# Self-attention of a fused block on one core: output projection behind the query projection, transposes ahead of the sums, and another order at both ends

## The chip, the cores and the metric

One core of one Trainium2 chip runs the whole block as one program. The metric is device time in microseconds (us), median of three executions. The engines are named as in the profile: PE (TensorE matmuls; PEld are its weight loads), DVE (VectorE), ACT (ScalarE), POOL (GpSimd) and SP (SyncE, which issues the transfers).

## The reference

The input x is 32 sequences of 32 tokens with 512 channels (1024 rows). Three layers follow each other, each added to x:

```python
x = x + xattn(layernorm(x), ctx, ctx)        # 16 heads of 32, 257 keys per sequence
x = x + attn(layernorm(x))                   # self-attention in each sequence of 32
x = x + ffn(layernorm(x))                    # nine experts, one chosen per token

# attn
q, k, v = x @ Wqkv.T + bqkv
q = rms_norm(q); k = rms_norm(k)             # per head: q / sqrt(mean(q*q) + 1e-6)
out = softmax(q k^T / sqrt(32)) v
return out @ Wproj.T + bproj

# ffn
x_mixed = mk[0]*x[s-1] + mk[1]*x[s] + mk[2]*x[s+1]
scores  = tanh(x_mixed @ Wo1 + bo1) @ Wo2 + bo2
path p  = (x_mixed @ W1[p] + b1[p]) @ W2[p] + b2[p]
return layernorm(x + the path with the highest score) * gamma + beta
```

All of it is float32. Each float32 product with 512 channels is made of three fp32r matmuls on operands that are split into a high and a low part (high times high, low times high, high times low).

## The kernel before, in words

**Tiles.** The 1024 rows are eight tiles of 128 rows (`NT` = 8); `NH` = 4 tiles are a half. `x_nat` keeps x in rows, `O_T` keeps the transposed output of cross-attention and later the mixed input of the experts. A projection of one tile (`project`, line 1094, by `three`, line 92) is 4 channel blocks of 3 matmuls of 128x512. "Splitting" means that ACT copies the high part (fp32r) and DVE or POOL subtracts it from the source, which gives the low part.

**Self-attention as a pipeline over turns.** After cross-attention `self_attention_and_experts` runs turns it = 0 to 7 and then some turns written out by hand (turn 8 is `NT`, turn 9 `NT + 1`, turn 10 `NT + 2`). In one turn every engine works on several tiles at once. PE (`body`, line 1206) does in this order: `wo_proj(it + 2)`, the output projection of cross-attention two tiles ahead (`LEAD` = 2, so only in turns 0 to 5); `out_proj(it)`, self-attention's output projection of tile it-3; `qk_transposes(it)`, of q and k of tile it-2, four transposes each; `qkv(it, 0)`, the query projection of tile it-1; `scores(it)` of tile it-2; `qkv(it, 1)` and `qkv(it, 2)`, keys and values; `weighted_sum(it)`; `z2_transposes(it)`, of the normalised x of tile it; `z3_transposes(it)`, of the input of the experts, tile it-3. Turn 2 projects the queries ahead of the q and k transposes.

**What else is in a turn.** Each engine runs its own instruction stream in program order, and they meet only at semaphores. DVE adds projections to x (`take_x1`, `take_x2`), takes the statistics of a layer norm (`x1_stats`, `x2_stats`), moves q, k and v out of PSUM with their bias, sums the squares of q and of k per head (`mean_squares`), multiplies q and k by their inverse norm (`head_norm(tile, 0)` for q, `head_norm(tile, 1)` for k; line 1613), does the softmax (`shift_scores`, `probabilities`) and the low parts `o2_split` and z2's. ACT makes the high parts, the normalised x (`z2_make`, `z3_make`), squares, exponentials, and `mix_parts`, the 12 scaled copies for the mixing of neighbours. POOL (line 1032) takes all inverse roots with a power instruction. Its order in a turn is: `head_norm(1, it-2)`, the roots for the keys (line 1012); `norm1(it)`; `o_rest(it+3)`; `norm3(it-3)`, which waits for `x2_stats(it)` and so for `out_proj(it)`; `with_bproj(it-1)`; `mix(it-4)`, two additions; `head_norm(0, it-1)`, the roots for the queries.

**Who waits for whom, around the change.** The second four transposes of `qk_transposes(it)` wait for `norm_made[1]`, the keys of tile it-2 multiplied on DVE, which waits for POOL's roots, which wait for `mean_squares(it-1, 1)`. On DVE that sum stands behind `head_norm(it-1, 0)` in turn it-1, which waits for POOL's roots for the queries. `out_proj(it)` waits for `o2_split(it-1)` on DVE. The first four transposes wait for z2's low part of tile it-1, since they write into the bank that z2's transposes used.

**Handover.** The weight of self-attention's output projection comes into `raw` while cross-attention's is in use. `weight_split(4)` on ACT and a subtraction of 128x2048 on DVE (line 1699) in turn 1 split it; `out_proj(3)` in turn 3 is its first use.

**Experts.** `gate(hf)` (line 1237) multiplies one half of the mixed input with the gate's weight. It needs `xm_hi`, `xm_lo` (the split mixed input of the half) and `g_hi`, `g_lo` (the split gate weight); POOL makes both low parts in turn 8 (lines 1066 and 1069). Then come `hidden(k)`, `spread(k)` (one matmul that spreads the chosen expert over the partitions, into the one bank `pw0`, evacuated by ACT in `spread_evac`), and `outputs`. The rest of self-attention (turns 9 and 10) is woven in.

**The end.** For the last four tiles DVE adds PE's result (`y_take`), takes statistics, centres and multiplies by gamma (two tiles; POOL does it for the other two, lines 1088 and 1090), takes all four inverse roots by a chain of twelve small instructions (`y_deviations`, `rsqrt`, line 50) and ends with four `y_end`; SP stores each tile.

## Time and profile before

| what | value |
|---|---|
| median of three executions | 794.98 us (794.23 to 797.06) |
| the profiled execution's own time | 793.65 us |
| its span | 791.7 us |
| PE busy | 751.6 us, 95% of the span |
| DVE, ACT, POOL busy | 390.5, 335.9, 187.7 us |
| cross-attention ends, self-attention begins | about 485 us |
| first matmul of the gate | 639.58 us |
| last matmul ends | 780.8 us |

How to read it: the span is the stretch from the first to the last instruction on the chip; the execution's own time is some 2 us more. PE is busy nearly all the time, so what matters are the few places in which it stands still, and what each of them waited for. PE's clock has two levels, 1.2 and 2.4 GHz; a granted clock of 1.00 in a row is the higher one, 0.50 the lower.

### The profile page before, as it was taken

What the parts mean: (1) busy time and instruction counts of PE and PEld (TensorE: products, weight loads), DVE (VectorE), ACT (ScalarE), POOL (GpSimd) and SP (SyncE); (2) the same over time, 40 slices, a digit from 0 to 9 for tenths busy, and PEclk for the clock granted to TensorE, in tenths of its full rate; (3) what the DMA queues carried; (4) which work ended last, traced back from release to release, by engine and by line L of the source; (5) the groups of instructions that cost most, each with busy time, mean ns of one, the idle gap of its engine ahead of it and who ended that gap; (6) DMA issues with size and microseconds to landing.
All of it is one profiled execution on the core that took longest, in us unless ns stands there. A gap on an engine that the chain in (4) does not pass through costs nothing. (4 is left out here: it accounts for less than half of the span.)

```text
span 791.7 us, 20456 instructions
## 1 busy us (share of the span) xinstructions
PE 751.6 (95%) x8258; PEld 587.8 (74%) x8258; DVE 390.5 (49%) x942; ACT 335.9 (42%) x690; POOL 187.7 (24%) x245
## 2 busy tenths in 40 slices
PE   5999999999999999999999999799999989999994
PEld 4777778778877877787788777677877766677673
DVE  5544434343443344243424546756667675633546
ACT  4435444443444344444435455224554545521210
POOL 0001000010010010010100202555777770692002
PEclk9999999999999999999999999999999999999998
DMA  9211110011011101101120114120000022100011
GB/s 331 71 48 55 54 55 23 33 53 53 0 53 53 53 0 53 53 1 52 53 49 4 53 53 108 66 84 3 0 0 4 2 69 80 41 1 0 1 54 53
DMA packets 9471, 37.05 MB, mean 47 GB/s; under 512 B 2633, under 2 KB 2889, under 8 KB 6482
## 3 DMA queue, kind: packets, MB, share of 16 engines
q1 hardware_dynamic: 9426, 36.42, 13.6%
q8 instruction: 31, 0.51, 0.3%
q14 instruction: 14, 0.11, 0.0%
HBM read 34.32 MB, written 2.10 MB: 46 GB/s over the span
## 5 line engine op out<-in xcount | busy, mean ns | idle before, releaser
L94 PE MATMUL pj<-W_hi 128*128 128x512 f32 x512 | 209.1, 408 | 9.7 <-DVE W_lo L594 9.7
L96 PE MATMUL pj<-W_lo,W_hi 128*128 128x512 f32 x512 | 201.2, 393 | 0.0
L95 PE MATMUL pj<-W_hi,W_lo 128*128 128x512 f32 x512 | 200.4, 391 | 0.0
L94 PEld LDWEIGHTS pj<-W_hi 128*128 128x128 f32 x512 | 96.8, 189 | 40.7 <-issue 22.4
L96 PEld LDWEIGHTS pj<-W_lo,W_hi 128*128 128x128 f32 x512 | 96.7, 189 | 21.4
L95 PEld LDWEIGHTS pj<-W_hi,W_lo 128*128 128x128 f32 x512 | 97.0, 189 | 17.9
L235 POOL COPY q_b<-Q_T 128x128 f32 (+1 forms) x32 | 9.3, 291 | 415.8 <-PE tp L358 348.9
L492 ACT ACTIVATE K<-pj,bk 128x512 f32<-128x512 f32 x64 | 44.1, 690 | 136.1 <-PE pj L96 136.1
L654 DVE CUSTOM_DVE_ANT_0 m_flat<-sc,mask 128x257 f32<-128x257 f32 x64 | 25.3, 425 | 115.4 <-PE tp L358 94.1
L507 ACT ACTIVATE p_flat<-m_flat,nmax 128x257 f32<-128x257 f32 x128 | 63.8, 501 | 24.5 <-DVE nmax L654 24.5
L499 ACT ACTIVATE V<-pj 128x512 f32<-128x512 f32 x64 | 38.2, 598 | 73.7 <-PE pj L96 71.8
L594 DVE TENSOR_TENSOR W_lo<-raw,W_hi 128x2048 fp32r<-128x2048 f32 (+1 forms) x19 | 41.4, 2180 | 31.4 <-ACT W_hi L451 31.4
L675 DVE COPY P_T<-tp 128x512 f32<-128x512 f32 x32 | 22.1, 692 | 66.6 <-PE tp L370 66.6
L1012 POOL TENSOR_TENSOR rms<-ms_eps,power 128x16 f32<-128x16 f32 x16 | 48.3, 3020 | 3.6 <-POOL ms_eps L1008 3.6
L663 DVE TENSOR_SCALAR p_flat<-p_flat,rinv 128x257 f32<-128x257 f32 x128 | 42.0, 392 | 1.1
L94 PE MATMUL pw<-W_hi,z_hi 128*128 128x512 f32 x92 | 38.0, 413 | 4.3 <-DVE x_nat L1565 4.3
L95 PE MATMUL pw<-W_hi,z_lo 128*128 128x512 f32 x92 | 36.4, 396 | 0.0
L96 PE MATMUL pw<-W_lo,z_hi 128*128 128x512 f32 x92 | 36.3, 395 | 0.0
L451 ACT ACTIVATE W_hi<-raw 128x2048 fp32r<-128x2048 f32 (+1 forms) x19 | 34.5, 1815 | 3.0 <-DMA raw<-wk_dram 3.0
L370 PE MATMUL tp<-ident,p_flat 128*128 128x128 f32 x256 | 33.1, 272 | 0.7 <-DVE P_T L675 0.7
L370 PEld LDWEIGHTS tp<-ident,p_flat 128*128 128x128 f32 x256 | 29.8, 140 | 4.8 <-issue 0.8
L94 PE MATMUL pt<-xm_hi,W_hi 128*128 128x512 f32 x72 | 29.1, 405 | 0.3 <-DVE bqkv L1737 0.3
(287 smaller groups left out, 1329.3 us busy)
## 6 DMA issues: line engine op xcount, KB each, us to landing
raw<-ctx_dram SPq DMA_DIRECT2D x15, 1024.0 KB, 4.8
raw<-w_dram SPq DMA_DIRECT2D x6, 768.0 KB, 4.9
raw<-w_dram SPq DMA_DIRECT2D x4, 1024.0 KB, 4.8
x_nat<-x_dram SPq DMA_DIRECT2D x2, 1024.0 KB, 11.7
out_dram<-raw SPq DMA_DIRECT2D x8, 256.0 KB, 2.1
raw<-wk_dram SPq DMA_DIRECT2D x2, 512.0 KB, 5.4
p_flat<-ctx_dram SPq DMA_DIRECT2D x2, 512.0 KB, 6.8
m_flat<-wv_dram SPq DMA_DIRECT2D x1, 1024.0 KB, 9.9
```

Of the source, the lines that this page charges most:

```text
L94: eng.matmul(out, a_hi, b_hi, start=first, stop=False)
L95: eng.matmul(out, a_lo, b_hi, start=False, stop=False)
L96: return eng.matmul(out, a_hi, b_lo, start=False, stop=last)
L370: mm = eng.transpose(tp[:, k, g * P:(g + 1) * P], probs[:, j, g, k * P:(k + 1) * P], ident[:, :])
L451: return eng.activation(dst, src, ACT.Copy)
L492: eng.activation(K[:, g, :, 0:SM], pj[g % 2][:, :].rearrange("p (j n) -> p j n", j=2), ACT.Identity, bias=bk[:, g:g + 1]).then_inc(k_out, 1)
L499: eng.activation(V[:, t, :], pj[t % 2][:, :], ACT.Copy).then_inc(v_out, 1)
L507: eng.activation(probs[:, j, g, :], masked[:, j, g, :], ACT.Exp, bias=nmax[:, j, g:g + 1], scale=-1.0, accum_out=psum_[:, j, g:g + 1]).the ...
L594: return eng.tensor_tensor(dst, src, hi.bitcast(F32), ALU.subtract)
L654: eng.tensor_tensor_reduce(masked[:, j, g, :], sc[g][:, 0:SK], mask[:, :], -1.0, BIG, ALU.add, ALU.min, nmax[:, j, g:g + 1]).then_inc(mask ...
L663: eng.tensor_scalar(probs[:, j, g, :], probs[:, j, g, :], rinv[:, j, g:g + 1], None, ALU.mult).then_inc(probs_made, 1)
L1012: eng.tensor_tensor(rms[:, heads], ms_eps[:, heads], power[:, heads], ALU.pow).then_inc(rms_made[i], 1)
```

## The change

Semaphores that only mark what an engine has seen are shared between the two stages (no wait hangs on them), and the unused count `x0_made` is dropped. Beyond that:

- **Turns.** PE does z2's transposes ahead of the weighted sum. In turns 6, 7 and 8, which have no `wo_proj`, `out_proj` stands behind `qk_transposes` and `qkv(it, 0)`. ACT and DVE split z2 ahead of o2. On DVE, `q_evac` stands ahead of `take_x2` in turns 6, 7 and 8.
- **Handover.** DVE's low part of Wproj moves from turn 1 to the end of turn 2, `head_norm(0, 0)` from turn 1 into turn 2 behind `take_x1` and `x1_stats`; ACT splits Wproj behind z2; PE waits for the low part at the end of turn 2.
- **Ahead of the experts.** The mixed input's first half is split tile by tile, on ACT at the end of turns 4 to 7 and on DVE at the end of turns 5 to 8; the gate's weight is split on ACT in turn 6 and on DVE in turn 7. POOL does neither. DVE's turns are written out instead of looped.
- **First experts.** `spread(0)` goes ahead of `weighted_sum(9)`, `out_proj(10)` behind `hidden(2)` and `spread(2)`; ACT and DVE take the evacuations for them ahead of weight splits.
- **End.** POOL takes each of the last four inverse roots by power; tiles 4 and 6 are normalised on ACT, multiplied by gamma on POOL, and added on POOL (4) and on DVE (6); tiles 5 and 7 stay on DVE. The stores follow in the order 4, 5, 7, 6.

The rest of the diff, in the order of the file (SP, POOL, PE, ACT, DVE):

```diff
...
-            for i, t in enumerate((0, 1, 2, 3, 6, 7, 4, 5)):
-                eng.wait_ge(fin, i + 1)
+            for t in range(NH):
+                eng.wait_ge(fin, t + 1)
+                eng.dma_start(out[t], y(t)).then_inc(stored, 16)
+            eng.wait_ge(fin0, 1)
+            eng.dma_start(out[NH], y(NH)).then_inc(stored, 16)
+            for i, t in enumerate((5, 7, 6)):
+                eng.wait_ge(fin, NH + i + 1)
                 eng.dma_start(out[t], y(t)).then_inc(stored, 16)
             eng.wait_ge(stored, 16 * NT)
...
@@ -1062,11 +1069,7 @@
             head_norm(1, NT - 2)
             norm3(NT - 3)
             mix(NT - 4)
-            eng.wait_ge(xmhi, 1)
-            eng.tensor_tensor(xm_lo[:, :, :], O_T[:, :, 0:HT], xm_hi[:, :, :].bitcast(F32), ALU.subtract).then_inc(xmlo, 1)
             head_norm(0, NT - 1)
-            eng.wait_ge(g_split, 1)
-            eng.tensor_tensor(g_lo[:, :, :], g_raw, g_hi[:, :, :].bitcast(F32), ALU.subtract).then_inc(g_split, 1)
             head_norm(1, NT - 1)
             with_bproj(NT - 1)
             norm3(NT - 2)
...
-            for t in range(2):
-                y_t = y(NH + t)
+            def y_root(t):
+                one = slice(t, t + 1)
                 eng.wait_ge(stats_made, NH + t + 1)
-                eng.tensor_scalar(y_t, y_t, mv4[:, t, 0:1], None, ALU.subtract).then_inc(centred, 1)
-                eng.wait_ge(centred, 2 * t + 1)
-                eng.tensor_tensor(y_t, y_t, gamma, ALU.mult).then_inc(centred, 1)
+                eng.tensor_scalar(tmp4[:, one], mv4[:, t, 1:2], LN_EPS, 1.0, ALU.add, ALU.mult).then_inc(root_step, 1)
+                eng.wait_ge(root_step, 2 * t + 1)
+                eng.tensor_tensor(rstd4[:, one], tmp4[:, one], power[:, one], ALU.pow).then_inc(root_step, 1)
+                eng.wait_ge(root_step, 2 * t + 2)
+                if t in (0, 2):
+                    eng.tensor_scalar(shift4[:, one], mv4[:, t, 0:1], rstd4[:, one], -1.0,
+                                      ALU.mult, ALU.mult).then_inc(shift4_made, 1)
+
+            def y_scale(t):
+                eng.wait_ge(normed, t // 2 + 1)
+                eng.tensor_tensor(y(NH + t), y(NH + t), gamma, ALU.mult).then_inc(centred, 1)
+
+            eng.wait_ge(fin, NH)
+            y_root(0)
+            y_scale(0)
+            y_root(1)
+            eng.wait_ge(centred, 1)
+            eng.tensor_tensor(y(NH), y(NH), x_nat[:, NH, :], ALU.add).then_inc(fin0, 1)
+            y_root(2)
+            y_root(3)
+            y_scale(2)
...
-                if isinstance(it, int) and it == 2 and i == 2:
-                    eng.wait_ge(wp_lo, 1)
...
-                if has(it, 3):
-                    out_proj(it)
+                    if has(it, 3):
+                        out_proj(it)
...
+                if not has(it, -LEAD):
+                    out_proj(it)
                 if has(it, 2):
                     scores(it)
                 if has(it, 1):
                     qkv(it, 1)
                     qkv(it, 2)
+                if not isinstance(it, int) or it >= 2:
+                    z2_transposes(it)
                 if has(it, 2):
                     weighted_sum(it)
-                if not isinstance(it, int) or it >= 2:
-                    z2_transposes(it)
+                if isinstance(it, int) and it == 2:
+                    eng.wait_ge(wp_lo, 1)
                 if has(it, 3):
                     z3_transposes(it)
...
@@ -1312,9 +1335,9 @@
 
             steps(eng, body)
 
-            out_proj(NT)
             qk_transposes(NT)
             qkv(NT, 0)
+            out_proj(NT)
             scores(NT)
             qkv(NT, 1)
             qkv(NT, 2)
...
@@ -1329,12 +1352,12 @@
             hidden(0)
             choice_transposes(0)
             hidden(1)
+            spread(0)
             weighted_sum(NT + 1)
-            spread(0)
             spread(1)
-            out_proj(NT + 2)
             hidden(2)
             spread(2)
+            out_proj(NT + 2)
             z3_transposes(NT + 1)
             expert(RING)
...
-                if has(it, 2):
-                    o2_split(it)
-                if isinstance(it, int) and it == 1:
-                    weight_split(4)
                 eng.wait_ge(z2T_done, it + 1)
                 need(eng, qkv_done, 3 * it)
                 eng.activation(z2_hi[:, :, :].rearrange("p c t -> p (c t)"), pt[0][:, :], ACT.Copy).then_inc(z2hi_made, 1)
+                if isinstance(it, int) and it == 1:
+                    weight_split(4)
+                if has(it, 2):
+                    o2_split(it)
                 if has(it, 3):
                     mix_parts(it)
...
-            def xm_split(hf):
-                eng.wait_ge(mix_made, NH * (hf + 1) + 1)
-                if hf:
-                    eng.wait_ge(h_done, E)
-                eng.activation(xm_hi[:, :, :], O_T[:, :, hf * HT:(hf + 1) * HT], ACT.Copy).then_inc(xmhi, 1)
+            def xm_split_tile(u):
+                cols = slice(u * P, (u + 1) * P)
+                eng.wait_ge(mix_made, u + 2)
+                eng.activation(xm_hi[:, :, cols], O_T[:, :, cols], ACT.Copy).then_inc(xmhi, 1)
+
+            def xm_split_rest():
+                eng.wait_ge(mix_made, NT + 1)
+                eng.wait_ge(h_done, E)
+                eng.activation(xm_hi[:, :, :], O_T[:, :, HT:T], ACT.Copy).then_inc(xmhi, 1)
+
+            def g_hi_split():
+                eng.wait_ge(ex_in, 6 * 16)
+                eng.activation(g_hi[:, :, :], g_raw, ACT.Copy).then_inc(g_split, 1)
...
+                if it >= NH:
+                    xm_split_tile(it - NH)
+                if it == NT - 2:
+                    g_hi_split()
...
-            xm_split(0)
             square(NT, 0)
             exps(NT)
-            eng.wait_ge(ex_in, 6 * 16)
-            eng.activation(g_hi[:, :, :], g_raw, ACT.Copy).then_inc(g_split, 1)
...
-            w_split(2)
+            spread_evac(0)
             o2_split(NT + 1)
-            z3_make(NT + 1)
-            spread_evac(0)
             hidden_split(0)
             spread_evac(1)
+            z3_make(NT + 1)
             hidden_split(1)
+            w_split(2)
+            spread_evac(2)
+            hidden_split(2)
...
-            spread_evac(2)
             mix_parts(NT + 1)
-            hidden_split(2)
             w_split(3)
...
                 hidden_split(k)
+            for t in (0, 2):
+                eng.wait_ge(shift4_made, t // 2 + 1)
+                eng.activation(y(NH + t), y(NH + t), ACT.Identity, bias=shift4[:, t:t + 1],
+                               scale=rstd4[:, t:t + 1]).then_inc(normed, 1)
...
+                if isinstance(it, int) and it == 2:
+                    head_norm(it - 2, 0)
                 if has(it, 2):
                     head_norm(it - 2, 1)
+                if not has(it, -LEAD):
+                    q_evac(it)
                 if has(it, 3):
                     take_x2(it)
                     x2_stats(it, ch)
-                if has(it, 1):
+                if has(it, 1) and has(it, -LEAD):
                     q_evac(it)
                 if has(it, 2):
                     shift_scores(it, ch)
@@ -1676,17 +1716,16 @@
...
-                    head_norm(it - 1, 0)
                 elif has(it, 1):
                     k_evac(it)
                     head_norm(it - 1, 0)
                     mean_squares(it, 1)
                     v_evac(it)
-                if has(it, 2):
-                    o2_split(it)
                 eng.wait_ge(z2hi_made, it + 1)
                 eng.tensor_tensor(z2_lo[:, :, :].rearrange("p c t -> p (c t)"), pt[0][:, :],
                                   z2_hi[:, :, :].rearrange("p c t -> p (c t)").bitcast(F32), ALU.subtract).then_inc(z2lo_made, 1)
+                if has(it, 2):
+                    o2_split(it)
...
-                if isinstance(it, int) and it == 1:
+                if isinstance(it, int) and it == 2:
                     eng.wait_ge(whi, 5)
                     eng.tensor_tensor(w_lo[4], raw[:, 0, :].rearrange("p (c n) -> p c n", c=CT), w_hi[4].bitcast(F32),
                                       ALU.subtract).then_inc(wp_lo, 1)
...
+            def xm_lo_tile(u):
+                cols = slice(u * P, (u + 1) * P)
+                eng.wait_ge(xmhi, u + 1)
+                eng.tensor_tensor(xm_lo[:, :, cols], O_T[:, :, cols], xm_hi[:, :, cols].bitcast(F32),
+                                  ALU.subtract).then_inc(xmlo, 1)
...
+            def hidden_made(k):
                 eng.wait_ge(pc_out, k + 1)
                 eng.wait_ge(h_done, k + 1)
                 need(eng, hlo, k - 1)
                 eng.scalar_tensor_tensor(out=h[k % 2], in0=ph(k)[:, :], scalar=b1[:, k % E:k % E + 1],
                                          in1=chosen[k % 2], op0=ALU.add, op1=ALU.mult).then_inc(h_made, 1)
+
+            def hidden_rest(k):
                 eng.wait_ge(hhi, k + 1)
                 eng.tensor_tensor(h_lo[k % RING], h[k % 2], h_hi[k % RING].bitcast(F32), ALU.subtract).then_inc(hlo, 1)
+
+            def hidden_rows(k):
+                hidden_made(k)
+                hidden_rest(k)
...
-            steps(eng, body)
+            for it in range(NT):
+                body(it)
+                if it > NH:
+                    xm_lo_tile(it - NH - 1)
+                if it == NT - 1:
+                    eng.wait_ge(g_split, 1)
+                    eng.tensor_tensor(g_lo[:, :, :], g_raw, g_hi[:, :, :].bitcast(F32), ALU.subtract).then_inc(g_split, 1)
             ch = Chain(eng, step, count["at"])
             head_norm(NT - 2, 1)
+            q_evac(NT)
             take_x2(NT)
             x2_stats(NT, ch)
-            q_evac(NT)
...
             v_evac(NT)
+            xm_lo_tile(NH - 1)
             o2_split(NT)
+            head_norm(NT - 1, 1)
             w_split(0)
-            head_norm(NT - 1, 1)
...
+            hidden_made(0)
             o2_split(NT + 1)
-            hidden_rows(0)
+            hidden_rest(0)
+            hidden_rows(1)
             w_split(2)
-            hidden_rows(1)
+            hidden_rows(2)
             take_x2(NT + 2)
             x2_stats(NT + 2, ch)
             eng.wait_ge(b2_split, 1)
             eng.tensor_tensor(b2_lo, b2, b2_hi.bitcast(F32), ALU.subtract).then_inc(b2_split, 1)
-            hidden_rows(2)
             w_split(3)
...
             for t in range(NH):
                 y_take(1, t)
                 y_stats(1, t)
-                if t == 2:
-                    y_centre(1, t)
-            y_centre(1, NH - 1)
-            y_deviations()
-            for t in (2, 3, 0, 1):
-                if t < 2:
-                    eng.wait_ge(centred, 2 * t + 2)
+                if t == 1:
+                    y_centre(1, 1)
+            y_centre(1, 3)
+            for t in (1, 3):
+                eng.wait_ge(root_step, 2 * t + 2)
                 y_end(1, t)
+            eng.wait_ge(centred, 2)
+            eng.tensor_tensor(y(NH + 2), y(NH + 2), x_nat[:, NH + 2, :], ALU.add).then_inc(fin, 1)
...
```

## Rows read from the trace of the kernel before

**Rows 1.** PE's waits, 484 to 670 us: total, times, longest.
```profile
PE pw L94 <- DVE x_nat L1565: 4.3, 1, 4.3
PE pw L94 <- DVE o_lo L1641: 4.3, 3, 1.4
PE pa L1190 <- DVE e_T L1637: 1.9, 1, 1.9
PE pw L1276 <- ACT sq L1486: 1.7, 1, 1.7
PE pw L94 <- POOL g_lo L1069: 1.4, 1, 1.4
```
**Rows 2.** Stretches: length, PE busy (instructions), granted clock, DMA share, GB/s.
```profile
513.40:517.70 4.30, 4.29 (x13) 0.65 0.53 112
...
589.70:592.60 2.90, 2.90 (x15) 1.00 0.00 0
...
659.70:664.20 4.50, 4.50 (x14) 0.62 0.28 105
```
**Rows 3.** PE in order of time, end of turn 6, turn 7: start, us, instruction.
```profile
603.21 0.51 PE L94 MATMUL pw<-Wp_hi,o_hi 128*128 128x512 f32 x1 [1.42 <-DVE o_lo L1641]
...
606.55 0.60 PE L1138 MATMUL pt<-ident,qk 128*128 128x128 f32 x4
606.90 0.48 PE L94 MATMUL pw<-W_hi,z_hi 128*128 128x512 f32 x1
```
**Rows 4.** DVE in order of time: turns 6 and 7.
```profile
588.53 0.69 DVE L1617 TENSOR_TENSOR qk<-qk,rms 128x512 f32<-128x512 f32 x1 [1.22 <-POOL rms L1012]
...
605.62 0.69 DVE L1617 TENSOR_TENSOR qk<-qk,rms 128x512 f32<-128x512 f32 x1 [0.91 <-POOL rms L1012]
606.41 0.69 DVE L1581 TENSOR_TENSOR x_nat<-pw,x_nat 128x512 f32<-128x512 f32 x1
...
608.12 0.18 DVE L1590 BATCH_NORM_AGGREGATE mv<-stats 128x2 f32<-128x6 f32 x1 [0.17 <-DVE stats L1587]
```
**Rows 5.** POOL in order of time: turn 6 and the start of turn 7.
```profile
591.24 0.19 POOL L981 TENSOR_SCALAR var_eps<-mv 128x1 f32<-128x1 f32 x1 [1.13 <-DVE mv L1590]
...
592.38 0.26 POOL L987 TENSOR_SCALAR shift<-mv,rstd 128x1 f32<-128x1 f32 x1 [0.21 <-POOL rstd L984]
...
592.84 1.27 POOL L1018 TENSOR_TENSOR x_nat<-x_nat,bproj 128x512 f32<-128x512 f32 x1
...
597.09 3.44 POOL L1012 TENSOR_TENSOR rms<-ms_eps,power 128x16 f32<-128x16 f32 x1 [0.21 <-POOL ms_eps L1008]
...
602.57 2.90 POOL L1012 TENSOR_TENSOR rms<-ms_eps,power 128x16 f32<-128x16 f32 x1 [0.21 <-POOL ms_eps L1008]
```
**Rows 6.** DVE, handover and turn 2; below it PE in turn 2.
```profile
510.38 2.28 DVE L1699 TENSOR_TENSOR Wp_lo<-raw,Wp_hi 128x2048 fp32r<-128x2048 f32 x1
...
529.10 0.68 DVE L1688 TENSOR_TENSOR z_lo<-pt,z_hi 128x512 fp32r<-128x512 f32 x1
...
527.71 0.66 PE L1107 MATMUL pt<-ident,z 128*128 128x128 f32 x4
```
**Rows 7.** DVE and POOL in turn 8.
```profile
632.03 3.07 DVE L1635 TENSOR_TENSOR e<-e,rs 128x512 f32<-128x512 f32 x1
...
629.96 4.59 POOL L1066 TENSOR_TENSOR xm_lo<-O_T,xm_hi 128x2048 fp32r<-128x2048 f32 x1
```
**Rows 8.** DVE, first experts: the last low part before the first outputs.
```profile
666.86 0.65 DVE L1805 TENSOR_TENSOR Wp_lo<-raw,Wp_hi 9x512 fp32r<-9x512 f32 x1
```
**Rows 9.** The end: DVE, and one multiplication by gamma on POOL.
```profile
778.04 1.29 POOL L1090 TENSOR_TENSOR raw<-raw,bproj 128x512 f32<-128x512 f32 x1
...
781.33 0.69 DVE L1749 TENSOR_TENSOR raw<-pa,raw 128x512 f32<-128x512 f32 x1
...
783.90 0.17 DVE L1765 TENSOR_SCALAR mv<-mv 128x4 f32<-128x4 f32 x1
...
786.29 2.74 DVE L1771 SCALAR_TENSOR_TENSOR raw<-raw,rstd,x_nat 128x512 f32<-128x512 f32 x4
```

More of the change, by code:

```diff
@@ L353, in scores @@
                     need(eng, pt_dve, 2 * n)
-                eng.sem_inc(s_ready, 1)
+                eng.sem_inc(pe_seen, 1)
                 for k in range(4):
@@ L813, in self_attention_and_experts @@
         small_in, scaled, wp_lo, ov_last = sem("small_in2"), sem("scaled"), sem("wp_lo"), sem("ov_last")
[L815 to L816 removed]
+        pe_seen, dve_seen, pool_seen = seen
+        ohi_made, olo_made, olo1_made = sem("ohi_made"), sem("olo_made"), sem("olo1_made")
         power_made = sem("power_made")
@@ L1238, in gate @@
                 eng.wait_ge(g_split, 2)
-                eng.wait_ge(xmlo, hf + 1)
+                eng.wait_ge(xmlo, NH + hf)
                 if hf == 0:
@@ L1539, in _ @@
                 hidden_split(k)
-            xm_split(1)
+            xm_split_rest()
             tanh(1)
@@ L1813, in _ @@
                 hidden_rows(e_)
-            eng.wait_ge(xmhi, 2)
+            eng.wait_ge(xmhi, NH + 1)
             eng.tensor_tensor(xm_lo[:, :, :], O_T[:, :, HT:T], xm_hi[:, :, :].bitcast(F32), ALU.subtract).then_inc(xmlo, 1)
```

25 lines of the change are left out of this document (12 added, 13 removed).

## The prediction

> **What bounds the kernel now.** I read the page first: PE is busy 95% of the span, so only its waits and what it repeats at the low clock can move the time. The second view is PE's waits [rows 1]: one of 4.3 us, of turn 2's query projection for x; three of 1.42 us for o2's low part ahead of the output projections of turns 6, 7 and 8; 1.9 us for the transposed probabilities in turn 8; 1.4 us for the gate weight's low part; 1.7 us for ACT's evacuation between two spreads. The third is PE's clock [rows 2]: a projection of 12 matmuls takes 2.9 us at 1.00, and 4.3 to 4.5 us at 0.65 and 0.62, that is partly at 1.2 GHz. Both slow ones follow a wait (the 4.3 and the 1.7 us). So a long wait is paid again with about 1.45 us. The last view is the order of time on PE, DVE and POOL in turns 6 and 7 [rows 3 to 5], which tells which wait would be next.
>
> **Turns 6, 7 and 8.** The 1.42 us waits go if PE has something else to do first. But what is put first is not ready. In turn 7 the output projection starts at 603.21 and fills PE until 606.11; the last four q/k transposes start at 606.55 and the query projection at 606.90 [rows 3]. They wait for the keys' multiplication on DVE, which ends at 605.62 + 0.69 = 606.31 [rows 4], right behind POOL's roots for the keys, 602.57 + 2.90 = 605.47 [rows 5]. This is no wait of PE in rows 1 only because the output projection covers it. In turn 6 the same multiplication ends at 588.53 + 0.69 = 589.22 [rows 4]. Nothing in the change makes it earlier. POOL's loop isn't touched.
>
> Worse, the loop now closes through the projection. POOL takes in one turn, in order: the roots for the keys; the third layer norm, which waits for x2's statistics and so for `out_proj(it)`; bias; mixing; the roots for the queries. With `out_proj` behind transposes and queries, everything behind the third norm starts later, the queries' roots too, and behind them on DVE the keys' squares, and next turn's keys. One round, from one end of `out_proj` to the next: 0.15 to DVE; take_x2 to the end of the aggregate 608.30 - 606.41 = 1.89 [rows 4]; 0.2 to POOL; third norm to the end of the queries' roots 597.09 + 3.44 - 591.24 = 9.29; to the start of the keys' roots 602.57 - 600.53 = 2.04, and 2.90 for them [rows 5]; 0.84 to the end of the keys' multiplication [rows 4, 5]; 0.59 to the query projection [rows 3, 4]; 2.95 for it and 2.95 for `out_proj` (2.9 in rows 2, in a stretch cut just inside the projection). Sum 23.8 us. Today a turn takes 605.62 - 588.53 = 17.1 us [rows 4]: 6.7 us more a round.
>
> In this trace's time: `out_proj(6)` would end at 589.22 + 0.59 + 5.9 = 595.7, `out_proj(7)` at 619.5, `out_proj(8)` at 643.3. From there to the gate: 0.15 + 1.89 + 0.2, then 9.29 less the bias of 1.27 that turn 8 lacks [rows 5], then DVE's multiplication of the queries, squares' sum, values' evacuation and last piece of `xm_lo`, 2.65 with the handovers (0.6 to 0.7 each, as the row of take_x2), and 0.1: 13.0. The gate starts at 656.3 instead of 639.58: **+16.7 us**. This holds already that the 1.42 us waits, the 1.9 and the 1.4 us are gone, and that POOL is rid of the 4.59 us of `xm_lo`, beside which DVE's multiplication took 3.07 instead of 0.69 [rows 7]. The added ACT copies and DVE pieces of a tile (0.6 to 0.7 us each) stand at the ends of turns, where both engines now wait for POOL; uncovered, three would cost 2 us.
>
> PE then stands still about 7 us ahead of the transposes in turns 7 and 8, longer than the 4.3 us after which the projection ran at 0.65. So 1.45 us each for both, on the loop; in turn 6 two waits of together some 4 us with four transposes between them, which I count half, 0.7: **+3.6 us**. Bounds for the three: 0 to 4.5.
>
> **Handover.** The 4.3 us were DVE's 2.28 us for Wproj's low part and the queries' multiplication ahead of `take_x1` [rows 1, 6]. Without them x is there 0.9 us after the projection: -3.4, and -1.45 for the clock. But PE now waits at the end of turn 2 for the moved 2.28 us. PE is through with sums and transposes at 528.37; DVE's part of the turn ends at 529.78 and the low part then at about 532.0 [rows 6], both earlier by the same gain. That is a new wait of 3.65 us, with 1.45 for the clock. Together **+0.25 us**; from -1.2 (clock stays up) to +1.5.
>
> **First experts.** Ahead of expert 3 the 1.7 us between the spreads go, and 1.6 for the clock [rows 1, 2]: the first evacuation by ACT stands ahead of o2 and a z3, and the weighted sum lies between the spreads. Given back: the low part of b2 ended at 667.51 just behind x2's last statistics [rows 8]; it now stands behind a weight split and a third hidden pair on DVE, I put it 1.8 us later, and PE is there earlier, so 0.9 to 1 us of waiting. **-2.3 us**, between -3.3 and 0.
>
> **End.** After PE's last matmul DVE takes the last tile at 781.33, starts the roots at 783.90, and ends at 786.29 + 2.74 = 789.03 [rows 9]. New: a root with its shift on POOL is 1.4 us (591.24 to 592.64, rows 5), without shift 0.95, a product with gamma 1.29 [rows 9], a pass of ACT taken as DVE's 0.7 to 0.8. POOL's queue from 776.4: root 4, ACT, gamma to 780.05; root 5 to 781.1; addition to 782.4; root 6 to 783.8; root 7 to 784.85; gamma to 786.3; DVE's addition to 787.15. **-1.9 us**, from -2.5 to 0.
>
> A rule speaks against this end. In turn 8, DVE's 3.07 us ended half a us behind POOL's 4.59 us [rows 7]: it stood still until POOL was through. The Trainium skill, page "SBUF — State Buffer", section "Who interferes with whom", says so in general: a DVE instruction with two inputs in SBUF and a GpSimd instruction that reads SBUF exclude each other for the whole instruction, whichever starts first; here the trace agrees, with 3.07 for 0.69. By it tile 7's `y_end` could hold back POOL's last product by some 0.7 us, and the end would gain 1.2.
>
> **Sum.** 16.7 + 3.6 + 0.25 - 2.3 - 1.9 = +16.35 us on the profiled execution's 793.65: **810 us**. The median shown is 1.3 us higher than that execution; I stay with 810.
>
> **Rivals.**
> 1. The clock stays up, or falls once: less by 2 to 4 us, 806 to 808. Against: both slow rows behind waits; for: a turn's wait is broken by four transposes.
> 2. The transposes are not held by the keys' roots in turns 6 to 8 (PE's waits name no such wait today). Then the edit does as meant: three times 1.42, 1.9, 1.4 with 1.45 of clock, 2.3 and 1.9 go: -13.2 with the handover's +0.25, so **780 to 781**, faster. It decides at the second four transposes of turn 6: the keys of tile 4 would have to be multiplied by 586 and not at 589.2. Against it: 605.62 and 588.53 in rows 4, both behind POOL.
> 3. Only the cover is lost and the loop isn't lengthened, because POOL would come to its third norm late anyway. Then transposes start as today, each turn has room for the 2.95 us (it now idles 1.42, and the waits of turn 8 go too), and the gate starts near 639.6: with the rest 789 to 791. Against: POOL waited 1.13 us for DVE's aggregate there already [rows 5].
> 4. The loop lengthens once only, since turn 8 has slack in another form: 800 to 804.
>
> **Numbers.** Forecast with its own range 807 to 814: 0.60; rival 1 below that: 0.14; rival 4: 0.07; rival 3: 0.06; rival 2: 0.07; above 814 (all clock falls in full, DVE and POOL in each other's way at each turn): 0.06. Low end 800, high end 816. Faster by over 0.5% (4 us, about what this measurement can tell): 0.08 (rival 2, and the edge of rival 3); within: 0.05 (the rest of rival 3); slower: 0.87.
>
> **What would show it.** After: PE's waits hold two of about 7 us and one of about 4 us ahead of q/k transposes, put down to DVE's multiplication of the keys, and none for o2's low part; a wait of 3.6 us at the end of turn 2; POOL's third norm starting behind `out_proj` in turns 6 to 8, its rounds some 24 us apart; granted clocks near 0.65 behind those waits; the gate starting 17 to 21 us later; the last store giving a span that ends about 9.0 us behind PE's last matmul instead of 10.9. I am wrong if the keys' multiplication in turn 7 comes before 608, or if the gate starts before 645.

## The result: 820 us, 3.1% slower than before

| | before | after |
|---|---|---|
| median of the four runs | 795.22 us (794.23 to 797.06) | 820.15 us (818.99 to 820.64) |
| ratio to before, 95% interval | 1 | 1.0314 [1.0299, 1.0328] |
| profiled execution, its span | 793.65, 791.7 | 820.64, 819.1 |
| mean granted clock of that execution | 0.99 | 0.966 |

The forecast was 810 with a range to 816, so the measured time lies 4 us above the range. Direction and place were right; the size was 10 us short. The 27.4 us of span came in this way:

| stretch | forecast | measured |
|---|---|---|
| before self-attention | 0 | -0.46 |
| turn 2 and the handover | +0.25 | +1.95 |
| turns 6 to 8, up to the gate | +20.3 | +23.0 |
| gate to the end of expert 3's hidden product | -2.3 | +1.7 |
| from there to PE's last matmul | 0 | +2.2 |
| behind PE's last matmul | -1.9 | -1.0 |

### The profile after

PE's waits from 475 to 700 us, in the trace of after (instruction, what it waited for: total us, times, longest). They answer to [rows 1].

```profile
PE pt L1159 <- DVE z_lo L1725: 7.3, 3, 3.1
PE pt L1159 <- DVE qk L1653: 6.9, 3, 2.8
PE pa L1209 <- DVE e_T L1673: 4.9, 3, 1.8
PE pw L95 <- DVE Wp_lo L1738: 4.5, 1, 4.5
PE pw L95 <- issue: 2.6, 1, 2.6
PE pw L1222 <- issue: 2.6, 1, 2.6
```

The waits for o2's low part are gone, as the change wants. In their place stand three kinds of three waits each, 19.1 us together, all in turns 6 to 8, and one of 4.5 us in turn 2. Of the two put down to "issue", the first stands ahead of the gate's first matmul at 664.09, just behind DVE's last piece of `xm_lo` (ended 663.99), and the second ahead of expert 3, which comes below. Stretches of after follow; beside what [rows 2] has they show every engine (length, busy time with instructions of PE, PEld, DVE, ACT and POOL, granted clock, DMA share, GB/s). The first is `wo_proj(5)`, cross-attention's output projection behind the 4.5 us; the other three are the query projections in turns 6, 7 and 8:

```profile
527.57:532.66 5.09, 5.09 (x13) 4.03 (x14) 0.00 (x0) 0.00 (x0) 0.00 (x0) 0.56 0.54 118
591.77:596.99 5.22, 5.22 (x15) 4.11 (x14) 0.00 (x0) 1.39 (x2) 0.07 (x1) 0.51 0.00 0
617.94:622.10 4.16, 4.16 (x15) 3.33 (x13) 0.00 (x0) 1.39 (x2) 0.07 (x1) 0.66 0.02 4
643.04:648.22 5.18, 5.18 (x14) 4.08 (x13) 0.00 (x0) 0.69 (x1) 0.00 (x0) 0.51 0.00 0
```

Each of these projections takes 2.9 us at 1.00 [rows 2]. Here they run at 0.51 to 0.66 and are 1.3 to 2.3 us longer. The end of turn 6 and turn 7 in order of time in after, PE first (start, us, engine, line, operation, output and inputs, in brackets the idle time before it and who ended it). It answers to [rows 3].

```profile
609.03 1.36 PE L1209 MATMUL pa<-e_T,v 32*32 32x32 f32 x128 [1.75 <-DVE e_T L1673]
...
614.02 1.11 PE L1159 MATMUL pt<-ident,qk 128*128 128x128 f32 x4 [2.75 <-DVE z_lo L1725]
617.18 1.11 PE L1159 MATMUL pt<-ident,qk 128*128 128x128 f32 x4 [2.04 <-DVE qk L1653]
617.94 0.78 PE L95 MATMUL pw<-W_hi,z_hi 128*128 128x512 f32 x1
...
624.67 0.39 PE L97 MATMUL pw<-Wp_lo,o_hi 128*128 128x512 f32 x1
```

DVE in the same stretch, against [rows 4]:

```profile
600.09 0.69 DVE L1617 TENSOR_TENSOR x_nat<-pw,x_nat 128x512 f32<-128x512 f32 x1 [2.21 <-PE pw L97]
...
601.80 0.18 DVE L1626 BATCH_NORM_AGGREGATE mv<-stats 128x2 f32<-128x6 f32 x1 [0.17 <-DVE stats L1623]
...
605.07 0.69 DVE L1646 TENSOR_REDUCE ms<-sq 128x16 f32<-128x512 f32 x1 [1.79 <-ACT sq L1428]
...
611.48 0.69 DVE L1653 TENSOR_TENSOR qk<-qk,rms 128x512 f32<-128x512 f32 x1 [2.01 <-POOL rms L1019]
...
613.28 0.68 DVE L1725 TENSOR_TENSOR z_lo<-pt,z_hi 128x512 fp32r<-128x512 f32 x1
...
616.43 0.69 DVE L1653 TENSOR_TENSOR qk<-qk,rms 128x512 f32<-128x512 f32 x1 [0.31 <-POOL rms L1019]
```

And POOL, against [rows 5]:

```profile
602.20 0.19 POOL L988 TENSOR_SCALAR var_eps<-mv 128x1 f32<-128x1 f32 x1 [10.36 <-DVE mv L1626]
...
603.80 1.30 POOL L1025 TENSOR_TENSOR x_nat<-x_nat,bproj 128x512 f32<-128x512 f32 x1
605.06 1.27 POOL L1034 TENSOR_TENSOR O_T<-O_T,o_b 128x496 f32<-128x496 f32 x1
606.51 1.09 POOL L1037 TENSOR_TENSOR O_T<-O_T,mixed 128x496 f32<-128x496 f32 x1 [0.18 <-POOL O_T L1034]
...
608.42 2.92 POOL L1019 TENSOR_TENSOR rms<-ms_eps,power 128x16 f32<-128x16 f32 x1 [0.21 <-POOL ms_eps L1015]
612.96 0.20 POOL L1015 TENSOR_SCALAR ms_eps<-ms 128x16 f32<-128x16 f32 x1 [1.63 <-DVE ms L1646]
613.38 2.91 POOL L1019 TENSOR_TENSOR rms<-ms_eps,power 128x16 f32<-128x16 f32 x1 [0.21 <-POOL ms_eps L1015]
```

Read the three together. POOL stood still for 10.36 us before its third norm, because `take_x2` on DVE (600.09) waits for `out_proj(6)` on PE. In the kernel before, POOL waited 1.13 us there [rows 5]. From 602.20 POOL is on the chain: norm, bias, two mixing additions, queries' roots, keys' roots to 616.29. DVE multiplies the keys at 616.43, PE transposes them, and only then come the query projection and `out_proj(7)`, which opens the next round. The same delay appears on PE under a further name: DVE's `z_lo` (613.28) reads nothing of POOL's, but stands behind the multiplication that waited for the queries' roots (611.48), and DVE takes its instructions in the order of the program. The wait for `e_T` (1.75 us ahead of the weighted sum at 609.03) has the same root. `take_x2` and its statistics (600.09 to 601.98) fall where DVE should take the scores, which end at 601.17; that is some 0.7 us. More comes behind it: DVE stands still 1.79 us ahead of 605.07 for ACT's squares of the queries. ACT squares them behind `z3_make`, and that waited 10.16 us for the shift of POOL's third norm, until 603.70. It isn't on the chain, since PE waits again right behind it.

Behind the gate, PE and DVE in after, ahead of expert 3:

```profile
692.06 0.70 PE L1222 MATMUL pw<-ident,z3s 128*128 128x128 f32 x4 [2.57 <-issue]
692.44 0.75 PE L95 MATMUL pt<-xm_hi,W_hi 128*128 128x512 f32 x1
```

```profile
687.55 1.76 DVE L1758 TENSOR_TENSOR W_lo<-raw,W_hi 128x1536 fp32r<-128x1536 f32 x1 [0.68 <-ACT W_hi L1488]
...
690.67 0.69 DVE L1787 TENSOR_TENSOR z_lo<-z,z_hi 128x512 fp32r<-128x512 f32 x1 [0.70 <-ACT z_hi L1522]
691.27 0.68 DVE L1617 TENSOR_TENSOR x_nat<-pw,x_nat 128x512 f32<-128x512 f32 x1
...
693.07 0.65 DVE L1865 TENSOR_TENSOR Wp_lo<-raw,Wp_hi 9x512 fp32r<-9x512 f32 x1
```

PE was through with `out_proj(10)` at 689.49. The next work in its queue, z3's transposes, writes a `pw` bank and in the kernel waits for `x2_made`, that is for `take_x2(10)`; that ran from 691.27 to 691.95, behind a weight split of 1.76 us and the third hidden pair, and the transposes follow at 692.06. So what the profile calls "issue" is here a wait for a bank to be read. Last, the end of after, against [rows 9]:

```profile
811.36 1.05 POOL L1093 TENSOR_TENSOR rstd<-tmp,power 128x1 f32<-128x1 f32 x1
...
813.91 1.82 POOL L1101 TENSOR_TENSOR raw<-raw,bproj 128x512 f32<-128x512 f32 x1
```

### The profile page after: what moved, and what is told of

It is laid out like the page before. It is cut to its first block and busy times, and to the rows that moved or that the text cites. A ratio compares the mean times of both kernels' runs of the same rounds, so it can differ in the third digit from the quotient of the medians.

```text
span 819.1 us, 20397 instructions
## 1 busy us (share of the span) xinstructions
PE 763.1 (93%) x8258; PEld 595.3 (73%) x8258; DVE 386.0 (47%) x934; ACT 338.1 (41%) x695; POOL 186.9 (23%) x252
## 5 line engine op out<-in xcount | busy, mean ns | idle before, releaser
L95 PE MATMUL pw<-W_hi,z_hi 128*128 128x512 f32 x92 | 39.9, 434 | 1.0 <-DVE x_nat L1601 1.0
L96 PE MATMUL pw<-W_hi,z_lo 128*128 128x512 f32 x92 | 38.3, 416 | 0.0
L97 PE MATMUL pw<-W_lo,z_hi 128*128 128x512 f32 x92 | 38.1, 414 | 0.0
```

What stands on the lines that cost most here:

```text
L95: eng.matmul(out, a_hi, b_hi, start=first, stop=False)
L96: eng.matmul(out, a_lo, b_hi, start=False, stop=False)
L97: return eng.matmul(out, a_hi, b_lo, start=False, stop=last)
```

## The experiments

Each kernel was timed beside the kernel before on the same chip; ratios are to it, with the 95% interval.

**Undo the one move, in the kernel after.** In turns 6 to 8 `out_proj` goes back ahead of the transposes, and `q_evac` behind `take_x2`.

```diff
@@ PE, the loop and turn 8
                     wo_proj(it + LEAD)
-                    if has(it, 3):
-                        out_proj(it)
+                if has(it, 3):
+                    out_proj(it)
...
-                if not has(it, -LEAD):
-                    out_proj(it)
...
+            out_proj(NT)
             qk_transposes(NT)
             qkv(NT, 0)
-            out_proj(NT)
```

> The changed kernel with one thing undone: in turns 6, 7 and 8 the output projection stands in front of the q/k transposes again (and DVE's q_evac behind take_x2). Theory (the loop closes through the output projection: third norm, mixing, roots for the queries, roots for the keys): the waits of the transposes in these turns go, the three 1.42 us waits for o2's low part come back, the gate starts 23 to 27 us earlier, time 793 to 797. Rival (only the cover of three projections of 2.95 us was lost, the rest of the loss comes from the splits by tile, z2 in front and DVE's order): 9 us less, 811.

Measured: 795.21 us, ratio 1.0003 [0.9989, 1.0016]. All 25 us hang on this one move, of `out_proj` on PE together with `q_evac` on DVE (neither half was tried alone), and the rest of the change adds up to nothing. PE's waits in it show where gains of the rest go:

```profile
PE pw L95 <- DVE o_lo L1675: 6.0, 3, 2.0
PE pw L95 <- DVE Wp_lo L1734: 4.5, 1, 4.5
PE pw L1222 <- issue: 2.6, 1, 2.6
```

The wait for o2's low part is 2.0 us a turn instead of 1.42 [rows 1], as o2 now stands behind z2's low part; the 4.3 us of turn 2 came back as 4.5; the 2.6 us is the bank of `take_x2(10)`. Behind three equal waits of 2.0 us the output projections took 3.06, 4.58 and 3.06 us: the same wait was paid again through the clock once, in turn 7, and not in turns 6 and 8.

**Do that one move alone, in the kernel before.** The mirror of the first diff.

> The kernel before with only that one thing done: output projection behind q/k transposes and query projection in turns 6, 7 and 8. Theory: 21 to 26 us slower than before, 816 to 821, with rounds of about 25 us between the ends of the output projections. Rival (cover only): three times 2.95, 804. Rival (the order is harmless alone and hurts only beside the split by tile on DVE and ACT): 795.

Measured: 820.35 us, ratio 1.0308 [1.0291, 1.0325]. PE's waits in it:

```profile
PE pa L1190 <- DVE e_T L1639: 9.7, 3, 5.4
PE pt L1138 <- DVE z_lo L1692: 6.4, 3, 2.2
PE pt L1138 <- DVE qk L1619: 5.6, 3, 2.2
```

`out_proj` ended at 598.60, 623.64 and 649.71: rounds of 25.04 and 26.07 us, in after 25.10 and 26.13. The move needs nothing else of the change to do all of its harm.

**Take the mixing off the chain, in the kernel after.** POOL's two mixing additions are cut from 496 columns to one for three tiles, which go unmixed into the experts.

```diff
                 eng.sem_inc(pool_seen, 1)
+                if 2 <= u <= 4:
+                    z, before, after = (a[:, 0:1, 0:1, :] for a in (z, before, after))
+                    left, right = slice(0, 1), slice(1, 2)
```

> The changed kernel with POOL's two mixing additions of turns 6, 7 and 8 cut to one column (three tiles go unmixed into the experts), 2.0 us less for POOL in each of these turns. After e6, in which POOL did the same work in another order and the rounds stayed at 26 us: theory: all that POOL does between the end of out_proj and the next keys (third norm, bias, mixing, both sets of roots) is serial, so only less of it helps: each of the three stretches of the chain (two rounds and the one to the gate) is 2 us shorter, time 6 to 7 us less, 813.5. Rival (the rounds hang on DVE and PE alone): no difference, 820.

Measured: 814.64 us, ratio 1.0252 [1.0233, 1.027]. Rounds were 23.28 and 23.56 us instead of 25.10 and 26.13, and the gate came 12.06 us behind `out_proj(8)` instead of 12.90. The query projections inside the two rounds took 4.37 and 4.66 us instead of 4.16 and 5.18; without them each round is 2.0 us shorter, which is what was cut. So what POOL does in a turn is paid in time: it is on the chain.

**The same cut in the kernel before.**

> The kernel before with the same cut as e9. Theory (the chain through POOL's whole turn already set the pace of turns 6 to 8 there, and the three 1.42 us waits for o2's low part are its excess over PE's 16 us of work): these waits go, with part of the 1.9 and 1.4 us of turn 8, 789 to 790. Rival (o2's low part is late for DVE's own reasons): 795.

Measured: 794.71 us (793.12 to 799.3), ratio 1.0005 [0.9988, 1.0021]: none of the gain of 5 us that I expected. Two of the three waits for o2's low part shrank, from 1.42 to 0.43 and 0.45 us, but later PE met a new one and ran slowly behind it:

```profile
671.94 0.37 PE L1279 MATMUL pw<-choice_b,sel 9*128 9x512 bf16 x1 [1.05 <-ACT sq L1489]
...
675.00 0.80 PE L94 MATMUL pa<-W_hi,o_hi 128*128 128x512 f32 x1
```

So POOL's mixing is on the path to these waits in the kernel before too: the rounds of turns 7 and 8 took 16.42 and 16.95 us instead of 17.39 and 17.25. Counted from the end of `out_proj(3)`, the gate started 1.2 us earlier than before. Then the gate's own product took 5.49 us instead of 4.49, behind the same two waits (1.95 and 1.5 us), and 1.0 of the 1.2 us were gone. The profiled execution is the slowest of the ten; from the end of expert 3's hidden product to the next z3 transposes, with the wait at 671.94, it took 4.9 us more than before. The ten times differ by 6 us with their mean clock (0.988 to 0.980), so whether 1 us of gain is left can't be told; 5 us can be excluded.

**Fill PE's waits, in the kernel after.** Spare matmuls before each of the two groups of transposes and before the weighted sum in turns 6 to 8, to keep the loop and take away the idle time, and with it the low clock.

```diff
+            def fill(n, bank):
+                for k in range(n):
+                    eng.matmul(bank, w_hi[4][:, k % CT, 0:P], w_hi[4][:, k % CT, P:D], start=True, stop=True)
...
+                late = isinstance(it, int) and NT - LEAD <= it <= NT
+                if late:
+                    eng.wait_ge(qk_out, 2 * (it - 1))
+                    fill(8, pw[0][:, P:D])
...
+                    if late and i == 1:
+                        fill(8, pw[0][:, P:D])
...
+                    fill(6, pa[:, 3, P:D])
```

> The changed kernel with 8 spare matmuls of 384 columns (about 0.17 us each) in front of each of the two waits of the q/k transposes, and 6 in front of the weighted sum, in turns 6, 7 and 8; they write into banks that nobody reads then, and lie inside the waits. Theory (the chain's waits are paid again through PE's clock, with 2.4, 1.4 and 2.4 us at the three query projections and 0.5 at each slow group of four transposes): granted clock 1.00 there, rounds of 23.5 to 24 us, time 6 to 9 us less, 811 to 814. Rival (the low clock costs nothing since the chain through DVE and POOL has slack there): 820. If the fill is late for what follows it, up to 2 us of this are lost.

Measured: 816.08 us (814.16 to 818.19), ratio 1.026 [1.0233, 1.0288]; 4.1 us less than after, and less of a gain than I expected. Turn 7 in order of time on PE:

```profile
610.83 2.51 PE L1153 MATMUL pw<-Wp_hi 128*128 128x384 f32 x8
613.13 1.05 PE L1169 MATMUL pt<-ident,qk 128*128 128x128 f32 x4
613.84 2.04 PE L1153 MATMUL pw<-Wp_hi 128*128 128x384 f32 x8
615.72 0.60 PE L1169 MATMUL pt<-ident,qk 128*128 128x128 f32 x4
616.08 0.47 PE L95 MATMUL pw<-W_hi,z_hi 128*128 128x512 f32 x1
```

The query projections took 2.98, 3.01 and 3.01 us instead of 5.2, 4.2 and 5.2. Rounds were 24.21 and 23.42 us. In turn 7 the spare matmuls ran to 615.88, while the keys were multiplied at 614.82, so 0.7 us of its round is the filling itself. The forecast without clock was 23.8, and 23.4 to 23.5 is left: the loop alone had been sized right to 0.4 us, and the rest of after's 25.1 and 26.1 is clock. Up to `out_proj(8)` and to the gate 5.9 us were gained. The two profiled executions differ by 5.2 us (820.64 and 815.40): between `out_proj(9)` and `out_proj(10)`, where PE stood still for 1.16 us inside the weighted sum, 1.4 us were lost again. The medians differ by 4.1, as each kernel's own runs spread by 2 to 4 us.

**Change POOL's order, in the kernel after.** Queries' roots ahead of third norm, bias and mixing; ACT's `z3_make` behind squares and splits.

```diff
+                if has(it, 1):
+                    head_norm(0, it - 1)
                 if has(it, 3):
...
                     mix(it - 4)
-                if has(it, 1):
-                    head_norm(0, it - 1)
```

> The changed kernel, output projection still behind, but POOL takes the roots for the queries of a turn ahead of the third norm, the bias and the mixing, and ACT makes z3 behind the squares and the splits of o2 and z2. Theory (the rounds of 25 us are a chain through the output projection, the third norm, 1.3 of bias, 2.5 of mixing and both sets of roots): the chain loses its 5.5 us of norm, bias and mixing but must still wait for the queries' squares on DVE, so rounds of 20 to 21.5 us in turns 6 to 8, the gate 11 to 15 us earlier, time 806 to 810. Rival (the rounds are set by the cover alone, that is by DVE and the keys' roots): rounds and time unchanged, 820.

Measured: 826.28 us, ratio 1.0394 [1.0375, 1.0414]: slower by 6 us where I expected 10 to 14 less. POOL in its turn 7:

```profile
613.04 2.92 POOL L1019 TENSOR_TENSOR rms<-ms_eps,power 128x16 f32<-128x16 f32 x1 [0.21 <-POOL ms_eps L1015]
616.04 0.19 POOL L988 TENSOR_SCALAR var_eps<-mv 128x1 f32<-128x1 f32 x1
...
620.53 1.31 POOL L1037 TENSOR_TENSOR O_T<-O_T,mixed 128x496 f32<-128x496 f32 x1 [0.18 <-POOL O_T L1034]
...
622.34 2.91 POOL L1019 TENSOR_TENSOR rms<-ms_eps,power 128x16 f32<-128x16 f32 x1 [0.21 <-POOL ms_eps L1015]
```

I had taken the queries' roots off the others' way and forgotten the keys': norm, bias and mixing now stand between the two pairs of roots (616.04 to 621.84), and PE waited 6.26, 6.41 and 5.90 us for the keys. Rounds were 26.23 and 26.88 us. All of a turn's work on POOL is still one string between two events of PE, whichever comes first. But the edit held in every turn and moved `z3_make` as well: PE waited 9.4 us in six turns for z3, which it never did in after, and the rounds of turns 4 and 5, outside the loop, grew by 4.0 and 1.5 us. So most of the loss against after isn't about the loop. The same order in the mended kernel below:

> e5 with POOL's and ACT's order of e6. Theory: the three waits of 1.4 us for o2's low part go too, since DVE's sums and splits of a turn stand behind the queries' roots; 4 us less than e5, 780. Rival (POOL's order matters only where the output projection stands behind): as e5. If z3 made later holds its transposes, up to 2 us are lost per turn and it is slower than e5.

Measured: 805.48 us, ratio 1.0137 [1.012, 1.0154], against 785.32 without it. Both causes are in its waits: 10.6 us in four for the keys, and 8.3 us in six for z3. How the 20 us divide between them was not tested.

**Put the wait where it is used.** PE waits for Wproj's low part inside `out_proj`, not ahead of `wo_proj` at the end of turn 2.

```diff
                 u = it - 3
+                eng.wait_ge(wp_lo, 1)
                 eng.wait_ge(o2lo_made, u + 1)
...
-                if isinstance(it, int) and it == 2:
-                    eng.wait_ge(wp_lo, 1)
```

> The changed kernel with PE's wait for Wproj's low part moved from the end of turn 2 to its first use, in front of out_proj(3), so that wo_proj(5) runs in its shadow. Theory (the handover's gain was given back by a wait that stands one projection too early): a wait of 1 to 1.5 us is left of 4.5, the clock stays up, 5 to 6 us less, 814.5. Rival (DVE's 2.28 us itself holds the chain, whoever waits): the wait moves to out_proj(3) or to take_x1(5) in full and the time stays at 820.

Measured: 814.99 us, ratio 1.0242 [1.0225, 1.0259], 5.2 us less than after. The wait left is this one. `wo_proj(5)`, now without a wait ahead of it, took 3.06 us instead of 5.09, and `out_proj(3)` behind the wait 3.04:

```profile
PE pw L95 <- DVE Wp_lo L1737: 1.3, 1, 1.3
```

So the 4.5 us stood ahead of a projection that doesn't read Wproj at all. At the end of `out_proj(3)` the gain is 4.3 us; the rest lies in the rounds of turns 6 to 8 (25.85, 24.72 and 25.92 instead of 26.58, 25.10 and 26.13), which the edit doesn't touch.

**z3's transposes behind expert 3's hidden product.**

```diff
             out_proj(NT + 2)
+            hidden(RING)
             z3_transposes(NT + 1)
-            expert(RING)
+            spread(RING)
+            for t in range(NH):
+                mm = outputs(0, t)
+            mm.then_inc(h_used, 1)
             z3_transposes(NT + 2)
```

> The changed kernel with one thing: z3_transposes(9) stands behind hidden(3) and no longer in front of it. Theory (PE's wait of 2.6 us there is for take_x2(10), which stands on DVE behind a weight split and the third hidden pair; it is paid again with 1.6 of clock): 4 us less, 816. Rival (the wait moves on to b2's low part or to hidden(3)'s weights): 818.5 to 820.

Measured in the kernel after: 821.12 us, ratio 1.0345 [1.0325, 1.0366]. Its runs fall in two groups, 816.05 and 816.5 us at a mean clock of 0.970 and 0.972, and three of 821.0 to 822.5 at 0.962 to 0.964; a sixth of 4083.24 us is left out. In the profiled one, of 816.5, PE needed 4.5 us less than in after from the gate to its last matmul, but the group of three shows no gain, so the times of this pair decide nothing. The same edit on the kernel of the first experiment, where the long waits of turns 6 to 8 are gone:

> e1 (changed kernel, output projection in front) with z3_transposes(9) behind hidden(3). e8 did this on the changed kernel, where its profiled execution was 4 us shorter and its median no shorter. Theory (the wait for take_x2(10) with its clock cost 4 us): 791 against e1's 795.2. Rival (the wait comes back elsewhere): 795.

Measured: 792.14 us, ratio 0.9976 [0.9957, 0.9995]; 3.1 us less than the 795.21 of the first experiment, and 2.1 us less by the two ratios, as the kernel before itself took 795.54 beside the one and 794.55 beside the other. The wait of 2.57 us is 0.65 there. So the bank's wait and the clock behind it are worth some 2 to 3 us.

**All mends together.** `out_proj` in front, the wait for Wproj at its use, z3's transposes behind the hidden product, and o2 summed and split ahead of z2 (PE, ACT and DVE).

```diff
@@ the fourth part, PE and DVE; ACT alike
-                if not isinstance(it, int) or it >= 2:
-                    z2_transposes(it)
                 if has(it, 2):
                     weighted_sum(it)
+                if not isinstance(it, int) or it >= 2:
+                    z2_transposes(it)
...
+                if has(it, 2):
+                    o2_split(it)
                 eng.wait_ge(z2hi_made, it + 1)
```

> The changed kernel with four things put right: output projection in front again in turns 6 to 8 (e1), PE's wait for Wproj's low part at its first use (e3), o2 summed and split ahead of z2 as before the change, and z3_transposes(9) behind hidden(3), so that PE does not stand still for take_x2(10). From e1's 795.2: 5.3 for the wait, 2.5 and 1.6 of clock for the transposes, 3 times 0.6 for o2 and 1.5 of the clock that fell in turn 7 there: 784, between 782 and 787, which beats both kernels. Rival (what is freed is lost at the next wait, as it was in e1, where several gains came to nothing): 791 or more.

Measured: **785.32 us** (782.55 to 789.59), ratio 0.9874 [0.9845, 0.9902]: it beats both kernels, by 1.3% and, by the two ratios, 4.3%. PE's waits in it:

```profile
PE pw L95 <- DVE o_lo L1678: 3.4, 3, 1.5
PE pw L95 <- DVE Wp_lo L1737: 1.1, 1, 1.1
```

From 795.2 to 785.3 are 9.9 us. Two parts were measured by themselves, each on another kernel than this: z3 with 3.1 and the wait with 5.2. That leaves 1.6 us for o2 ahead of z2, less than this kernel's runs differ among themselves, so that part isn't shown.

## Where the prediction was right, and which steps failed

**The loop through the projection: right, step by step.** One round, from the end of `out_proj(6)` at 599.96 to that of `out_proj(7)` at 625.06:

| step | forecast | after |
|---|---|---|
| `take_x2`, statistics, to POOL | 2.24 | 2.24 |
| third norm to the end of the queries' roots | 9.29 | 9.14 |
| to the end of the keys' roots | 4.94 | 4.95 |
| keys' multiplication ends | 0.84 | 0.83 |
| to the query projection | 0.59 | 0.82 |
| query projection | 2.95 | 4.16 |
| `out_proj(7)` | 2.95 | 2.96 |
| round | 23.8 | 25.1 |

The first four rows hold to 0.15 us, and the gate came 12.90 us behind `out_proj(8)` (forecast 13.0). What the prediction called the cover of the keys' wait [rows 3, 4] was real: the undone move gives back all of it, the move alone takes all of it, and shortening POOL shortens the rounds.

What failed is the sizing of the sum: five of its terms were too low. The largest miss is the give-back at the first experts (4.0 us, with the wrong wait named), the next the clock's price in turns 6 to 8 (2.7), then a stretch that was put at nothing (2.2), the handover (1.7) and the end (0.9).

**The clock in turns 6 to 8: the mechanism right, the term mis-sized.** I had +3.6 us with 4.5 as the upper bound. The slow query projections and the transposes ahead of them cost 2.5, 1.4 and 2.5 us in turns 6, 7 and 8, as each round stands over its forecast without clock: 6.4. Turn 7 was as priced. In turns 6 and 8 the projection took 5.2 us, and not the 4.3 to 4.5 of rows 2. The bound was no bound: it was the cost behind the one long wait of 4.3 us, and here waits follow each other with only four or eight transposes and one weighted sum between them. I counted turn 6's broken wait half, and it was paid in full. That a broken wait can be paid in full stood in the trace of before. I had read that only two slow products follow a wait, and missed a third, the gate's:

```profile
635.99 1.57 PE L1190 MATMUL pa<-e_T,v 32*32 32x32 f32 x128 [1.95 <-DVE e_T L1637]
...
639.58 0.79 PE L94 MATMUL pw<-xm_hi,g_hi 128*128 128x512 f32 x1 [1.43 <-POOL g_lo L1069]
```

Behind these two waits, with a weighted sum and four transposes between them, the gate's 12 matmuls took 4.49 us, at a granted clock of 0.65. With the waits filled the rounds are 24.2 and 23.4, so the excess was the clock and not a longer loop.

**The waits I named.** I wrote of two waits of about 7 us for the keys, and of 4 us in two pieces in turn 6. Ahead of the query projection of turn 6 stand 1.42 and 2.80 us, ahead of that of turn 7 1.75, 2.75 and 2.04, and ahead of that of turn 8 1.76, 3.12 and 2.04: 4.2, 6.5 and 6.9 together, the last two in three pieces under three names. Their sums were right; that the long ones would break up was not seen, and I should have asked where else PE meets DVE's queue in such a turn.

**The handover: +0.25 forecast, +1.95 measured.** The direction of both parts was right: the 4.3 us went, and the same split of Wproj was met at the end of turn 2, 4.53 us instead of 3.65. The projection behind it took 5.09 us, 2.1 over its 2.95 where I had 1.45. So the two terms were small by 0.9 and 0.7. What I had not asked is whether the instruction behind the wait needs the data. It doesn't; moving the wait saved 5.2 us.

**The first experts: -2.3 forecast, +1.7 measured, the wrong wait and the largest miss.** The gain came: the 1.66 us between the spreads are gone, and `out_proj(10)` took 3.07 us instead of 4.61. I looked for the give-back at b2's low part, which I had as late by 0.9 to 1 us. It was earlier, at z3's transposes: 2.57 us for `take_x2(10)`, with 4.60 us instead of 3.05 for expert 3's hidden product. The gate's product at the head of this stretch took 5.08 us instead of 4.49, for which I had no term. I had moved DVE's weight split and third hidden pair ahead of b2's split in my mind, but not ahead of `take_x2(10)`, which stands before it in the same queue.

**From there to the last matmul: 0 forecast, +2.2 measured.** PE waited 1.1 us at 739.88 before a gate, where DVE's rest of `xm_lo` took 2.97 us beside a POOL instruction of 4.13, and the twelfth hidden product, `hidden(11)`, took 4.24 us at a granted clock of 0.68. In before it took 3.07 behind the same two short waits (0.78 and 0.32 us); why the clock was lower this time stays open. I had put this stretch at nothing without a reason.

**The end: -1.9 forecast, -1.0 measured.** The last product with gamma on POOL took 1.82 us and not 1.29 [rows 9], a root 1.05 and not the 0.55 of the next one, each beside a DVE instruction of 0.75 us with two inputs in SBUF. The estimate by the Trainium skill's page "SBUF — State Buffer", section "Who interferes with whom", was -1.2, and was the nearer. The trace agrees: both of POOL's instructions were lengthened by 0.5 us.

Together: 2.7 us from the clock in turns 6 to 8, 1.7 from the handover, 4.0 from the first experts, 2.2 from the later ones, 0.9 from the end, less 0.5 at the start: 11.0, which is 27.4 less the forecast 16.35. But for the start, all errors lie on one side. I had taken each as its own small risk, though some 6.7 us of the 11 are one thing, PE at the low clock: 2.7 in turns 6 to 8, 0.7 at the handover, 0.6 at the gate, 1.5 at expert 3 and 1.2 at `hidden(11)`, all but the last behind a new or longer wait. One slip changes nothing in the forecast: rival 2's -13.2 us is its sum without the handover's +0.25, which still gives 780 to 781.

## What to carry to other kernels

A wait that the profile doesn't list may be covered by the very instruction that one wants to move: before moving it, find when the inputs of what comes next are ready, and whether the moved work feeds them a turn later, since then the delay is paid once a round. Put a wait ahead of the instruction that uses the data, and a consumer that frees a bank ahead of long work in its engine's queue. Price a new wait of several us with its clock at the worst the trace has shown, and look through the whole trace for slow products behind waits that work breaks up, not only behind the longest wait. Treat several terms priced so as one risk, not as independent ones.

## What the runs showed of the hardware that was not expected

- Behind waits of 1.4 to 3.1 us that followed each other with a few transposes between them, a projection of 12 matmuls took 4.2 to 5.2 us at a granted clock of 0.51 to 0.66 instead of 2.9 at 1.00. With spare matmuls in these waits it took 2.98 to 3.01.
- The same wait is not always paid again: in the first experiment the projections behind three waits of 2.0 us took 3.06, 4.58 and 3.06 us.
- One and the same kernel differs from run to run with its mean granted clock: the mended one 782.6 us at 0.996, 783.7 at 0.993, 787.0 at 0.992 and 789.6 at 0.986. A gain of 1 to 2 us can't be told from this in a few runs, as with the cut of the mixing in the kernel before.
- POOL's last 128x512 product took 1.82 us beside DVE's two-input instruction instead of 1.29, and DVE's multiplication of the probabilities 1.47 us instead of 0.69 beside POOL's additions.
